# A decoder on one Trainium2 core: a new order of a block's work on all five queues, and the norms of queries and keys inverted one by one

## The chip, the cores and the metric

One core of a Trainium2 chip. The metric is the device time of one launch, in microseconds (us). The engines are TensorE (PE; its weight loads are PEld), VectorE (DVE), ScalarE (ACT), GpSimd (POOL) and SyncE (SP, which only issues DMAs). Each works through its own queue in order, and they meet at semaphores.

## The reference, cut to what matters

Three residual parts on x of shape (4, 512, 128): gated linear attention, cross attention, and a decoder of six layers. The change lies in the decoder. All in float32.

```
for i in range(6):
    x = attn_layer(shift_tokens(x), Wqkv[i], q_scale[i], k_scale[i], Wo[i]) + x
    x = ffn_layer(shift_tokens(x), ln_g[i], ln_b[i], W1[i], b1[i], W2[i], b2[i]) + x

attn_layer: q, k, v = split(x @ Wqkv)             # 16 heads of 64
            q = l2norm(q) * qs; k = l2norm(k) * ks # x / max(|x|, 1e-12), per head
            q, k = rotary(q), rotary(k)
            out = softmax(8 q k^T, masked) v       # windows of 32, this one and the last
            return out @ Wo
ffn_layer:  xn = layernorm(x) * g + b
            a, gate = split(xn @ W1 + b1)          # 341 each
            return a * gelu(gate) @ W2 + b2
```

## The kernel before, in words

The decoder works on blocks of 128 tokens: 4 blocks in a batch entry, 4 entries, 6 layers, so 96 blocks. `step(g, ...)` exists once for each engine and is called for g = 0 to 98. A step works on four blocks at once, as a pipeline: part a on block g (project, square, rotate and scale queries and keys), part b on block g-1 (values, turned keys and queries, scores and their maximum), part c on block g-2 (exponential, sums, turned weights, weighted values), part d on block g-3 (turn the heads' output). n = g % 4, and the entry that is four or more blocks behind is in its FFN: at n = 2 and 3 the output projection (`project_out`), at n = 0 the norm (`centre`, `variance`), at n = 1 the hidden layer (`hid_gate`, `hid_value`, `gelu`, `gated`, three chunks of 128, 128 and 85 channels), at n = 2 the second product (`ffn_project`, `update`). The FFN of entry f = g // 4 - 2 runs for g from 8 on. After the last step, `finish` does the last entry's FFN.

PSUM has four double banks: bank_x (values, then scores), bank_y (turned heads, turned keys, the keys' projection, weighted values), bank_z (the queries' projection, turned queries, turned weights), bank_f (the FFN). Each is used several times in a step, so an operation waits both for its inputs and for the last reader of its bank.

The order on PE in a step before: queries' projection (L683, through `project`, L609), values (L690), heads turned (L694, through `turn`, L613), FFN work, keys turned, queries turned (L709, L713), keys' projection (L718), half of the scores (L666), turned weights, the other half, FFN work, half of the weighing (L673), FFN work, the other half, and at n = 1 the third hidden chunk (L758). Waits there that matter: the keys' turn waits for POOL's product (`k_normed`) and for ACT's copy of the turned heads (`heads_turned_copied`); the queries' turn for `q_normed` and, since it overwrites bank_z, for DVE's rotation of the new queries (`q_sin`); the keys' projection for ACT's copy of the turned keys (`k_turned_copied`); the weighing for `k_sin`.

On ACT before: exponential of block g-2 (L958), at n = 1 the norm's affine (L944), square of the queries (L965), copy of the values (L970), of the turned heads (L977), mask (L981), at n = 0 the FFN's square (L932), at n = 1 the load of the GELU table (L985), copies of turned keys and queries (L990, L992), square of the keys (L1003), copy of the turned weights (L1008), at n = 0 the FFN's inverse spread (L936, L938), copy of the weighed heads (`copy_heads`, L950), and last both norms' logarithm and exponential in one pair of 32 columns (L1020, L1024). A norm is inverted as exp(-0.5 ln(max(sum, 1e-24))). At n = 1 the three GELUs (L926) lie between, and the load of the table of logarithm and exponential (L1017) before L1020.

On DVE before: row sums and reciprocal (L1126, L1130), rotation of the queries (`rotary`, L1080 and L1083, which first waits until POOL is done with the last block's queries, `q_normed`), their sum of squares (L1119), FFN work, rotation of the keys, maximum and shift of the scores (L1151, L1155), the keys' sum, and one clamp of both (L1162); then at n = 0 `norm` (L1108), at n = 3 `add_projected` (L1095 to L1101).

On POOL before: scaled weights (L1387), the queries' rotated sum (L1392), the next block's shifted tokens (`stage`, L1374, L1377), the keys' rotated sum (L1399), and then both products with the inverse norms (L1405), queries first.

SP issues the copies of the values into windows (`windows`, L354) when `values_copied` comes, and reloads weights at layer ends.

Of the kernel before, what the change touches and what calls it, by code (L numbers as in the profile page):

```python
# [7 lines left out]
PARTS = 128  # L8
# [21 lines left out]
def decoder(nc, io, LAYERS=6):  # L30
# [39 lines left out]
    sq_sums = sb('SS', [PARTS, 2, 16])  # L70
# [98 lines left out]
    sums_clamped = nc.alloc_semaphore('sums_clamped')  # L169
    norms_log = nc.alloc_semaphore('norms_log')  # L170
    inverse_norms = nc.alloc_semaphore('inverse_norms')
# [130 lines left out]
    alpha_w_loaded = nc.alloc_semaphore('alpha_w_loaded')  # L302
    HIDDEN_CHUNKS = [128, 128, 85]
# [11 lines left out]
    with nc.Block() as block:  # L315

        @block.sync
        def _(sp):
# [47 lines left out]
            sp.wait_ge(zeroed, 6)  # L366
# [27 lines left out]
        def _(pe):  # L394
# [221 lines left out]
            def hid_gate(k, R):  # L616
                M = HIDDEN_CHUNKS[k]
                mm(R[0:M, 0, :], w_1[:, 341 + k * 128:341 + k * 128 + M], ffn_in[:, :], start=True, stop=True)  # L618
# [37 lines left out]
            def step(g, n, a, b, c, d, f, fo):  # L656
# [19 lines left out]
                if a:  # L676
# [7 lines left out]
                    project(bank_z, w_q, 1, n).then_inc(q_projected, 1)  # L684
                if b:
# [62 lines left out]
                if f is not None and n == 1:  # L748
                    hid_value(1, bank_f)
# [48 lines left out]
        def _(act):  # L798
# [121 lines left out]
            def gelu(f, k, R):  # L920
                M = HIDDEN_CHUNKS[k]
                act.wait_ge(hidden_ready, 3 * f + k + 1)
# [17 lines left out]
            def ffn_affine(f):  # L940
                act.wait_ge(ffn_normed, f + 1)
                if due(f):
                    act.wait_ge(hidden_ready, 3 * f)
                A(ffn_in[:, :], normed[:, :], ACT.Identity, scale=layer_vecs[:, f // 4 * 9 + 6:f // 4 * 9 + 7], bias=layer_vecs[:, f // 4 * 9 + 7:f // 4 * 9 + 8]).then_inc(ffn_input, 1)  # L944

            def copy_heads(g):
# [3 lines left out]
                A(heads.rearrange('p (c q d) -> p q c d', q=2, d=64), bank_y.rearrange('p q (c d) -> p q c d', d=64), ACT.Copy).then_inc(heads_copied, 1)  # L950

            def step(g, n, a, b, c, d, f, fo):
# [6 lines left out]
                if f is not None and n == 1:  # L959
                    ffn_affine(f)  # L960
# [5 lines left out]
                if b:  # L966
                    act.wait_ge(values_ready, g)
                    if due(g - 1):
                        act.wait_ge(windows_loaded, 160 * (g - 1))
                    A(v_rows[:, (n - 1) % 2, :], flat(bank_x), ACT.Copy).then_inc(values_copied, 1)  # L970
                if d:
# [5 lines left out]
                    A(heads_t[:, :, slot * 128:slot * 128 + 128], turned(bank_y), ACT.Copy).then_inc(heads_turned_copied, 1)  # L977
                if b:
# [3 lines left out]
                if f is not None and n == 0:  # L982
                    square(f)
                if f is not None and n == 1:
                    nc.scalar.preload_act_table_set(GELU)  # L985
                if b:
# [3 lines left out]
                    A(k_t[:, :, 32 + 128 * par:160 + 128 * par], turned(bank_y), ACT.Copy).then_inc(k_turned_copied, 1)  # L990
                    act.wait_ge(q_turned, g)
                    A(q_t[:, :, :], turned(bank_z), ACT.Copy).then_inc(q_turned_copied, 1)  # L992
                    if n == 2:

                        act.wait_ge(k_turned_copied, g)
                        A(k_t[:, :, 0:32], k_t[:, :, 256:288], ACT.Copy).then_inc(keys_carried, 1)
                if f is not None and n == 1:
                    gelu(f, 0, bank_f)
                if a:
# [9 lines left out]
                if f is not None and n == 0:  # L1009
                    inverse(f)  # L1010
                if f is not None and n == 1:
                    gelu(f, 1, bank_f)
                if c:
                    copy_heads(g)
                if f is not None and n == 1:
                    gelu(f, 2, bank_f)
                    nc.scalar.preload_act_table_set(LNEXP)  # L1017
                if a:
                    act.wait_ge(sums_clamped, g + 1)
                    A(norm_logs[:, :], sq_clamped[:, :], ACT.Ln).then_inc(norms_log, 1)  # L1020
                    act.wait_ge(norms_log, g + 1)
                    if due(g):
                        act.wait_ge(k_normed, g)
                    A(inv_norms[:, :, :].rearrange('p a b -> p (a b)'), norm_logs[:, :], ACT.Exp, scale=-0.5).then_inc(inverse_norms, 1)  # L1024
# [11 lines left out]
            def finish():  # L1036
# [9 lines left out]
                ffn_affine(f)  # L1046
# [6 lines left out]
            act.wait_ge(zeroed, 6)  # L1053
# [8 lines left out]
        def _(dve):  # L1062
# [7 lines left out]
            def gated(f, k, R):  # L1070
                M = HIDDEN_CHUNKS[k]
                dve.wait_ge(gate_gelu, 3 * f + k + 1)
                if k == 0:
# [30 lines left out]
            def norm(f):  # L1104
                dve.wait_ge(ffn_inverse, f + 1)
                if due(f):
                    dve.wait_ge(ffn_input, f)
                V.tensor_tensor(normed[:, :], bank_f[:, 1, :], spread[:, :], ALU.mult).then_inc(ffn_normed, 1)  # L1108
# [6 lines left out]
            def sums(j, squared, done, g):  # L1115
# [377 lines left out]
```

## Time and profile before

| | |
|---|---|
| median of 3 runs | 2223.14 us (2221.44 to 2223.32) |
| the profiled execution | 2225.41 us, span 2223.6 us |
| PE busy | 2016.6 us, 91% of the span |
| DVE, ACT, POOL busy | 1359.7 (61%), 1357.9 (61%), 1079.4 us (49%) |
| mean granted TensorE clock | 0.984 |

The profile covers one execution. Its span runs from the first to the last instruction; its own time is 1.8 us longer. In the timeline a row merges like instructions that follow each other: its start is the first one's, its length reaches to the end of the last, and idle time in brackets lies ahead of it with what ended it. The end of a matmul is modelled and overlaps the next start, so distances are taken from start to start. A wait counts only where the waiting engine is what the others wait for.

### The profile page before, as it was taken

How to read it: one execution, taken by the hardware profiler on the slowest of the kernel's cores; microseconds unless marked ns; L12 is line 12 of the kernel's file. 1: busy time of each engine (PE TensorE's matmuls, PEld its weight loads, DVE VectorE, ACT ScalarE, POOL GpSimd, SP SyncE). 2: the span in 40 equal slices, each digit the busy share in tenths (PEclk: the TensorE clock that was granted, in tenths of full speed). 3: DMA queues.
4: the chain of work that ended last, by engine and by line, in shares of the span. 5: the costliest groups of instructions: out<-in, count | busy, mean ns of one | idle time of the engine just before them, and what ended most of it. 6: DMA issues, size and time to landing. Idle time of an engine off the chain costs nothing.

```text
span 2223.6 us, 73529 instructions
## 1 busy us (share of the span) xinstructions
PE 2016.6 (91%) x32616; PEld 1195.3 (54%) x32616; DVE 1359.7 (61%) x1663; ACT 1357.9 (61%) x1669; POOL 1079.4 (49%) x708
## 2 busy tenths in 40 slices
PE   8999997789999999999999999999999999999987
PEld 5655654355555555555555555555555555555553
DVE  1454454666666666666667666666666676667662
ACT  5556553456666666666666666666666666666664
POOL 0000000576555655565556555655555556556640
PEclk9999997799999999999999999999999999999999
DMA  3000000122223222232222322222322223222220
GB/s 105 1 1 1 1 20 29 39 59 59 59 60 86 68 68 59 59 89 69 67 59 69 86 59 76 72 57 69 78 70 68 59 59 88 68 69 59 59 59 19
DMA packets 82055, 128.02 MB, mean 58 GB/s; under 512 B 17230, under 2 KB 28108, under 8 KB 81740
## 3 DMA queue, kind: packets, MB, share of 16 engines
q1 hardware_dynamic: 81740, 123.33, 21.4%
q8 instruction: 258, 4.23, 0.8%
q14 instruction: 57, 0.47, 0.1%
HBM read 21.55 MB, written 1.05 MB: 10 GB/s over the span
## 4 chain that ended last, share of the span: by engine, by line
PE 64%; ACT 16%; issue 8%; DVE 7%; POOL 4%; DMA 0%; POOLq 0%; ACTq 0%; SPq 0%; DVEq 0%
PE ps L609 14%; PE ps L613 8%; PE ps L635 7%; PE ps L673 5%; PE ps L690 5%; PE ps L666 5%; ACT KT L990 4%; PE ps L422 3%; PE ps L653 3%; PE ps L618 2%; PE ps L622 2%; POOL work L1405 2%; DVE work L1083 2%; DVE work L1080 2%; ACT ps L981 2%
## 5 line engine op out<-in xcount | busy, mean ns | idle before, releaser
L1405 POOL TENSOR_TENSOR work<-work,RS 128x1024 f32<-128x1024 f32 x192 | 361.6, 1904 | 312.4 <-ACT RS L1024 312.4
L613 PEld LDWEIGHTS ps<-ident,work 128*128 128x128 f32 x3072 | 346.8, 142 | 150.6 <-issue 71.0
L1080 DVE TENSOR_TENSOR work<-ps,work 128x1024 f32<-128x1024 f32 x192 | 230.7, 1202 | 314.3 <-ACT work L1003 303.0
L613 PE MATMUL ps<-ident,work 128*128 128x128 f32 x3072 | 396.6, 277 | 27.9 <-POOL work L1405 12.5
L1399 POOL TENSOR_TENSOR work<-work 128x1024 f32<-128x1024 f32 x96 | 226.2, 2356 | 372.8 <-DVE work L1083 372.8
L609 PE MATMUL ps<-WK,XS 128*128 128x512 f32 x384 | 190.8, 620 | 50.0 <-ACT KT L990 49.8
L1083 DVE TENSOR_TENSOR work<-ps,work 128x1024 f32<-128x1024 f32 x192 | 233.0, 1214 | 0.0
L1119 DVE TENSOR_REDUCE SS<-work 128x16 f32<-128x1024 f32 x192 | 232.0, 1209 | 0.0
L1392 POOL TENSOR_TENSOR work<-work 128x1024 f32<-128x1024 f32 x96 | 226.1, 2356 | 5.7 <-DVE work L1083 5.7
L950 ACT ACTIVATE work<-ps 128x1024 f32<-128x1024 f32 x96 | 98.1, 1022 | 210.0 <-PE ps L673 208.2
L673 PEld LDWEIGHTS ps<-work 64*32 64x32 f32 x12288 | 135.4, 105 | 165.4 <-issue 109.2
L673 PE MATMUL ps<-work 64*32 64x64 f32 x12288 | 171.5, 224 | 33.9 <-DVE work L1083 18.0
L609 PE MATMUL ps<-WQ,XS 128*128 128x512 f32 x384 | 193.3, 626 | 8.5 <-POOL XS L1377 4.3
L635 PE MATMUL ps<-work,WO 128*128 128x512 f32 x384 | 193.3, 617 | 0.0
L1126 DVE TENSOR_REDUCE LE<-work 128x16 f32<-128x1024 f32 x96 | 116.9, 1218 | 123.5 <-ACT work L958 123.2
L666 PEld LDWEIGHTS ps<-KT,work 64*32 64x32 f32 x12288 | 135.9, 105 | 104.6 <-issue 102.9
L1387 POOL TENSOR_TENSOR work<-work,RL 128x1024 f32<-128x1024 f32 x96 | 182.9, 1905 | 11.9 <-DVE RL L1130 11.9
L690 PE MATMUL ps<-WV,XS 128*128 128x512 f32 x384 | 181.8, 596 | 2.5 <-DVE work L1155 2.5
L666 PE MATMUL ps<-KT,work 64*32 64x64 f32 x12288 | 171.1, 224 | 11.8 <-issue 11.4
L1003 ACT ACTIVATE work<-ps 128x1024 f32<-128x1024 f32 x96 | 98.5, 1026 | 95.5 <-PE ps L609 95.5
L1417 POOL TENSOR_TENSOR work<-work 128x512 f32<-128x512 f32 x16 | 16.5, 1041 | 273.7 <-PE ps L456 148.1
L1076 DVE SCALAR_TENSOR_TENSOR work<-ps,vec,work 128x512 f32<-128x512 f32 (+1 forms) x72 | 53.8, 747 | 150.4 <-ACT work L926 150.4
(183 smaller groups left out, 3097.8 us busy)
## 6 DMA issues: line engine op xcount, KB each, us to landing
work<-work SPq DMA_DIRECT2D x576, 128.0 KB
work<-work SPq DMA_DIRECT2D x336, 64.0 KB
WQ<-in_wqkv SPq DMA_DIRECT2D x6, 512.0 KB, 3.6
WK<-in_wqkv SPq DMA_DIRECT2D x6, 512.0 KB, 4.0
WV<-in_wqkv SPq DMA_DIRECT2D x6, 512.0 KB, 3.7
WO<-in_wo SPq DMA_DIRECT2D x6, 512.0 KB, 3.9
work<-ZR SPq DMA_DIRECT2D x48, 64.0 KB
W<-in_w SPq DMA_DIRECT2D x6, 341.0 KB, 3.0
```

The costliest lines, as they stand in the source:

```text
L609: return mm(R[:, half, :], x_shift[:, 32 + at * 128:160 + at * 128], w[:, half * 512:half * 512 + 512], start=True, stop=True)
L613: m = nc.tensor.transpose(flat(R)[:, t * 128:t * 128 + 128], src[:, t * 128:t * 128 + 128], ident[:, :])
L635: m = mm(bank_f[:, 0, :], w_o[:, k, :], heads_t[:, k, 128 * (f % 2):128 * (f % 2) + 512], start=k == 0, stop=k == 7)
L666: m = mm(bank_x[32 * w:32 * w + 32, q, c8 * 64:c8 * 64 + 64], q_t[64 * q:64 * q + 64, c8, 32 * w:32 * w + 32], k_t[64 * q:64 * q + 64, c8, ...
L673: m = mm(bank_y[32 * w:32 * w + 32, q, c8 * 64:c8 * 64 + 64], probs_t[64 * q:64 * q + 64, c8, 32 * w:32 * w + 32], v_win[64 * q:64 * q + 6 ...
L690: m = mm(bank_x[:, q, :].rearrange('p (c d) -> p c d', d=64), x_shift[:, 32 + nb * 128:160 + nb * 128], w_v[:, :].rearrange('p (c q d) -> ...
L1080: V.tensor_tensor(h16(cos_part[:, j, :]), h16(flat(src)), rotary_tabs[:, at:at + 64].unsqueeze(1).broadcast_to([PARTS, 16, 64]), ALU.mult) ...
L1083: V.tensor_tensor(halves(sin_part[:, j, :]), halves(flat(src))[:, :, ::-1, :], rotary_tabs[:, at + 256:at + 320].rearrange('p (s d) -> p s ...
L1119: V.tensor_reduce(sq_sums[:, j, :], h16(squares[:, j, :]), AX, ALU.add).then_inc(done, 1)
L1392: U.tensor_tensor(cos_part[:, 0, :], cos_part[:, 0, :], sin_part[:, 0, :], ALU.add).then_inc(q_rotated, 1)
L1399: U.tensor_tensor(cos_part[:, 1, :], cos_part[:, 1, :], sin_part[:, 1, :], ALU.add).then_inc(k_rotated, 1)
L1405: U.tensor_tensor(h16(qk_norm[:, j, :]), h16(cos_part[:, j, :]), inv_norms[:, j, :].unsqueeze(2).broadcast_to([PARTS, 16, 64]), ALU.mult). ...
```

## The change

PE: the heads are turned before the values are projected, and the keys are turned right after the values, ahead of the FFN work; the queries' turn and the keys' projection stay behind it. At n = 1 the second hidden chunk's gate and value are done together, the third chunk's gate goes between the halves of the weighing (with a wait for the second GELU), its value stays last. The GELU waits for the gate's product alone. ACT: the inversion of the norms is split in two, each of 16 columns; the queries' goes ahead of the keys' square (at n = 1 with an FFN: into the next step, behind the copy of the turned heads), the keys' goes ahead of `copy_heads`, except at n = 1; the copy of the turned heads goes ahead of that of the values; the GELU table is loaded behind the copy of the turned keys; at n = 0 the FFN's inverse goes last. The norm's affine goes from ACT to DVE. DVE: each clamp is a maximum over pairs (sum, 1e-24), done right after its sum; at n = 1 the second `gated` goes behind the scores' shift. POOL: the queries' product goes ahead of the keys' rotated sum (at n = 1 with an FFN: behind the keys' product). SP issues what it did, in the same order.

```diff
@@ PE @@
+                if d:
+                    pe.wait_ge(heads_copied, g - 2)
+                    turn(bank_y, heads).then_inc(heads_turned, 1)
                 if b:
...
                     m.then_inc(values_ready, 1)
-                if d:
-                    pe.wait_ge(heads_copied, g - 2)
-                    turn(bank_y, heads).then_inc(heads_turned, 1)
+                if b:
+                    pe.wait_ge(k_normed, g)
+                    if d:
+                        pe.wait_ge(heads_turned_copied, g - 2)
+                    turn(bank_y, qk_norm[:, 1, :]).then_inc(k_turned, 1)
                 if f is not None and n == 0:
                     centre(f)
...
                 if b:
-                    pe.wait_ge(k_normed, g)
-                    if d:
-                        pe.wait_ge(heads_turned_copied, g - 2)
-                    turn(bank_y, qk_norm[:, 1, :]).then_inc(k_turned, 1)
                     if a:
                         pe.wait_ge(q_sin, g + 1)
...
                     pe.wait_ge(hidden_gated, 3 * f + 1)
-                    hid_gate(1, bank_f)
+                    hid(1, bank_f)
...
-                    hid_value(1, bank_f)
+                    pe.wait_ge(gate_gelu, 3 * f + 2)
+                    hid_gate(2, bank_f)
...
                     pe.wait_ge(hidden_gated, 3 * f + 2)
-                    hid(2, bank_f)
+                    hid_value(2, bank_f)
@@ ACT @@
+            def invert_norms(g, j):
+                clamped, logs, inverse_done, normed_ = ((q_clamped, q_norms_log, q_inverse, q_normed), (k_clamped, k_norms_log, k_inverse, k_normed))[j]
+                act.wait_ge(clamped, g + 1)
+                A(norm_logs[:, 16 * j:16 * j + 16], sq_clamped[:, 16 * j:16 * j + 16], ACT.Ln).then_inc(logs, 1)
...
+                A(inv_norms[:, j, :], norm_logs[:, 16 * j:16 * j + 16], ACT.Exp, scale=-0.5).then_inc(inverse_done, 1)
...
-                if f is not None and n == 1:
-                    ffn_affine(f)
...
+                if n == 2 and f is not None and g - 1 < ALL_BLOCKS:
+                    invert_norms(g - 1, 0)
+                if b:
+                    act.wait_ge(values_ready, g)
...
                 if f is not None and n == 1:
                     gelu(f, 0, bank_f)
+                elif a:
+                    invert_norms(g, 0)
                 if a:
                     act.wait_ge(k_projected, g + 1)
...
                 if f is not None and n == 1:
                     gelu(f, 1, bank_f)
+                    gelu(f, 2, bank_f)
                     copy_heads(g)
                     nc.scalar.preload_act_table_set(LNEXP)
+                    if a:
+                        invert_norms(g, 1)
+                elif f is not None and n == 0:
+                    if c:
+                        copy_heads(g)
+                    if a:
+                        invert_norms(g, 1)
+                    inverse(f)
+                else:
+                    if a:
+                        invert_norms(g, 1)
+                    if c:
+                        copy_heads(g)
@@ DVE @@
-                V.tensor_tensor(normed[:, :], bank_f[:, 1, :], spread[:, :], ALU.mult).then_inc(ffn_normed, 1)
+                V.scalar_tensor_tensor(out=bank_f[:, 0, :], in0=bank_f[:, 1, :], scalar=layer_vecs[:, f // 4 * 9 + 6:f // 4 * 9 + 7], in1=spread[:, :], op0=ALU.mult, op1=ALU.mult).then_inc(ffn_normed, 1)
+                dve.wait_ge(ffn_normed, f + 1)
+                V.tensor_scalar(ffn_in[:, :], bank_f[:, 0, :], layer_vecs[:, f // 4 * 9 + 7:f // 4 * 9 + 8], None, ALU.add).then_inc(ffn_input, 1)
...
-                V.tensor_reduce(sq_sums[:, j, :], h16(squares[:, j, :]), AX, ALU.add).then_inc(done, 1)
+                V.tensor_reduce(sq_sums[:, j, :, 0], h16(squares[:, j, :]), AX, ALU.add).then_inc(done, 1)
+                dve.wait_ge(done, g + 1)
+                if due(g):
+                    dve.wait_ge(logs, g)
+                V.tensor_reduce(sq_clamped[:, 16 * j:16 * j + 16], sq_sums[:, j, :, :], AX, ALU.max).then_inc(clamped, 1)
@@ POOL @@
+                    late = f is not None and n == 1
+                    if not late:
+                        norm_product(g, 0)
                     pool.wait_ge(k_cos, g + 1)
...
+                    norm_product(g, 1)
+                    if late:
+                        norm_product(g, 0)
```

`norm_product(g, j)` is the body of the old loop at L1405 with the wait on the half's own inverse. One more constant is set at the start (1e-24 beside each sum).

## Rows read from the trace of the kernel before

**Rows 1.** The page: the chain that ended last, by engine.
```profile
PE 64%; ACT 16%; issue 8%; DVE 7%; POOL 4%; DMA 0%; POOLq 0%; ACTq 0%; SPq 0%; DVEq 0%
```
**Rows 2.** A wait over the whole span: waiter, releaser, us in total, times, longest.
```profile
PE ps L609 <- ACT KT L990: 49.8, 83, 1.3
```
**Rows 3.** Timeline of PE: start us, us, engine, line, out<-in, xcount, idle before.
```profile
645.79 1.88 PE L609 MATMUL ps<-WQ,XS 128*128 128x512 f32 x4
...
1161.62 1.88 PE L609 MATMUL ps<-WQ,XS 128*128 128x512 f32 x4
...
1170.75 1.96 PE L609 MATMUL ps<-WK,XS 128*128 128x512 f32 x4 [0.33 <-ACT KT L990]
...
1179.78 1.98 PE L609 MATMUL ps<-WQ,XS 128*128 128x512 f32 x4
...
1183.31 1.04 PE L613 MATMUL ps<-ident,work 128*128 128x128 f32 x8
...
1197.18 1.98 PE L609 MATMUL ps<-WQ,XS 128*128 128x512 f32 x4
...
1204.33 1.09 PE L613 MATMUL ps<-ident,work 128*128 128x128 f32 x8 [0.26 <-DVE work L1083]
1205.35 1.96 PE L609 MATMUL ps<-WK,XS 128*128 128x512 f32 x4
...
1210.81 0.86 PE L673 MATMUL ps<-work 64*32 64x64 f32 x64 [0.73 <-DVE work L1083]
...
1213.82 1.98 PE L609 MATMUL ps<-WQ,XS 128*128 128x512 f32 x4
...
1223.19 1.96 PE L609 MATMUL ps<-WK,XS 128*128 128x512 f32 x4 [1.32 <-ACT KT L990]
...
1232.20 1.09 PE L618 MATMUL ps<-YN,W 128*85 128x512 f32 x2 [0.78 <-DVE work L1076]
...
1233.99 1.88 PE L609 MATMUL ps<-WQ,XS 128*128 128x512 f32 x4
...
2115.00 1.88 PE L609 MATMUL ps<-WQ,XS 128*128 128x512 f32 x4
```
**Rows 4.** Timeline of ACT around the starts of steps.
```profile
1197.29 1.02 ACT L950 ACTIVATE work<-ps 128x1024 f32<-128x1024 f32 x1 [3.45 <-PE ps L673]
...
1212.76 0.69 ACT L936 ACTIVATE YQ<-ps,tiny 128x512 f32<-128x512 f32 x1 [2.58 <-PE ps L647]
...
1214.02 1.00 ACT L950 ACTIVATE work<-ps 128x1024 f32<-128x1024 f32 x1
...
1234.89 1.28 ACT L1017 ACT_TABLE_LOAD   x1
1236.19 0.23 ACT L1020 ACTIVATE LS<-SL 128x32 f32<-128x32 f32 x1
...
1236.58 1.04 ACT L958 ACTIVATE work<-work 128x1024 f32<-128x1024 f32 x1
...
1238.43 1.02 ACT L970 ACTIVATE work<-ps 128x1024 f32<-128x1024 f32 x1
```
**Rows 5.** Timeline of DVE: clamps, and from the row sums to the queries' rotation.
```profile
1182.49 1.22 DVE L1126 TENSOR_REDUCE LE<-work 128x16 f32<-128x1024 f32 x1 [2.55 <-ACT work L958]
...
1185.00 1.21 DVE L1083 TENSOR_TENSOR work<-ps,work 128x1024 f32<-128x1024 f32 x1
...
1198.02 0.18 DVE L1162 TENSOR_SCALAR SL<-SS 128x32 f32<-128x32 f32 x1
...
1214.36 0.18 DVE L1162 TENSOR_SCALAR SL<-SS 128x32 f32<-128x32 f32 x1
```
**Rows 6.** Timeline of POOL: the two norm products of a step.
```profile
1236.75 3.77 POOL L1405 TENSOR_TENSOR work<-work,RS 128x1024 f32<-128x1024 f32 x2 [5.63 <-ACT RS L1024]
```
**Rows 7.** Groups by line over the span: mean ns of one, then idle before.
```profile
L1113 DVE SCALAR_TENSOR_TENSOR X<-ps,vec,X 128x512 f32<-128x512 f32 x24 | 17.8, 742 | 6.6 <-PE ps L653 6.6
```
**Rows 8.** Timeline of PE in step 6, where the clock fell.
```profile
502.85 3.50 PE L613 MATMUL ps<-ident,work 128*128 128x128 f32 x16 [2.17 <-POOL work L1405]
```

More of the change, by code:

```diff
@@ L981, in step @@
                     A(bank_x.rearrange('p q (c k) -> p (q c) k', k=64), seed.unsqueeze(1).broadcast_to([PARTS, 16, 64]), ACT.Copy).then_inc(mask_seeded, 1)
[L982 to L985, printed above, removed]
                 if b:
@@ L990, in step @@
                     A(k_t[:, :, 32 + 128 * par:160 + 128 * par], turned(bank_y), ACT.Copy).then_inc(k_turned_copied, 1)
+                if f is not None and n == 1:
+                    nc.scalar.preload_act_table_set(GELU)
+                if b:
                     act.wait_ge(q_turned, g)
@@ L996, in step @@
                         A(k_t[:, :, 0:32], k_t[:, :, 256:288], ACT.Copy).then_inc(keys_carried, 1)
+                if f is not None and n == 0:
+                    square(f)
                 if f is not None and n == 1:
                     gelu(f, 0, bank_f)
+                elif a:
+                    invert_norms(g, 0)
                 if a:
@@ L1113, in update, with sums @@
                 V.scalar_tensor_tensor(out=xc, in0=bank_f[:, 1, :], scalar=layer_vecs[:, f // 4 * 9 + 8:f // 4 * 9 + 9], in1=xc, op0=ALU.add, op1=ALU.add).then_inc(x_updated, 1)
-            def sums(j, squared, done, g):
+            def sums(j, g):
+                squared, done, clamped, logs = ((q_squared, q_sums, q_clamped, q_norms_log), (k_squared, k_sums, k_clamped, k_norms_log))[j]
                 dve.wait_ge(squared, g + 1)
                 if due(g):
-                    dve.wait_ge(sums_clamped, g)
-                V.tensor_reduce(sq_sums[:, j, :], h16(squares[:, j, :]), AX, ALU.add).then_inc(done, 1)
+                    dve.wait_ge(clamped, g)
+                V.tensor_reduce(sq_sums[:, j, :, 0], h16(squares[:, j, :]), AX, ALU.add).then_inc(done, 1)
+                dve.wait_ge(done, g + 1)
+                if due(g):
+                    dve.wait_ge(logs, g)
+                V.tensor_reduce(sq_clamped[:, 16 * j:16 * j + 16], sq_sums[:, j, :, :], AX, ALU.max).then_inc(clamped, 1)
             def step(g, n, a, b, c, d, f, fo):
@@ L1136, in step @@
                     rotary(g, n, 0, bank_z, q_cos, q_sin, q_rotated)
-                    sums(0, q_squared, q_sums, g)
+                    sums(0, g)
                 if f is not None and n == 2:
@@ L1146, in step @@
                     rotary(g, n, 1, bank_y, k_cos, k_sin, k_rotated)
-                if f is not None and n == 1:
-                    gated(f, 1, bank_f)
                 if b:
@@ L1155, in step @@
                     V.tensor_tensor(scores_sb[:, :, :, :], by_head(bank_x), per_head(row_max[:, :]).unsqueeze(3).broadcast_to([PARTS, 8, 2, 64]), ALU.subtract).then_inc(scores_shifted, 1)
+                if f is not None and n == 1:
+                    gated(f, 1, bank_f)
                 if a:
-                    sums(1, k_squared, k_sums, g)
-                    dve.wait_ge(q_sums, g + 1)
-                    dve.wait_ge(k_sums, g + 1)
-                    if due(g):
-                        dve.wait_ge(norms_log, g)
-                    V.tensor_scalar(sq_clamped[:, :], sq_sums[:, :, :].rearrange('p a b -> p (a b)'), 1e-24, None, ALU.max).then_inc(sums_clamped, 1)
+                    sums(1, g)
                 if f is not None and n == 0:
@@ L1351, in _ @@
             cross()
+            dve.wait_ge(zeroed, 7)
             for g in range(ALL_BLOCKS + 3):
@@ L1381, in scale_tables, with norm_product @@
                 U.tensor_tensor(t, rotary_base[:, :, :, :], qk_scales[:, :, layer, :].unsqueeze(2).broadcast_to([PARTS, 4, 4, 64]), ALU.mult).then_inc(tables_scaled, 1)
+            def norm_product(g, j):
+                inverse_done, turned, rotated, normed_ = ((q_inverse, q_turned, q_rotated, q_normed), (k_inverse, k_turned, k_rotated, k_normed))[j]
+                pool.wait_ge(inverse_done, g + 1)
+                pool.wait_ge(rotated, g + 1)
+                if due(g):
+                    pool.wait_ge(turned, g)
+                U.tensor_tensor(h16(qk_norm[:, j, :]), h16(cos_part[:, j, :]), inv_norms[:, j, :].unsqueeze(2).broadcast_to([PARTS, 16, 64]), ALU.mult).then_inc(normed_, 1)
             def step(g, n, a, b, c, d, f, fo):
@@ L1399, in step @@
                     U.tensor_tensor(cos_part[:, 1, :], cos_part[:, 1, :], sin_part[:, 1, :], ALU.add).then_inc(k_rotated, 1)
-                    for j, (turned, rotated, normed_) in enumerate(((q_turned, q_rotated, q_normed), (k_turned, k_rotated, k_normed))):
-                        pool.wait_ge(inverse_norms, g + 1)
-                        pool.wait_ge(rotated, g + 1)
-                        if due(g):
-                            pool.wait_ge(turned, g)
-                        U.tensor_tensor(h16(qk_norm[:, j, :]), h16(cos_part[:, j, :]), inv_norms[:, j, :].unsqueeze(2).broadcast_to([PARTS, 16, 64]), ALU.mult).then_inc(normed_, 1)
+                    norm_product(g, 1)
+                    if late:
+                        norm_product(g, 0)
             def attention():
```

55 lines of the change are left out of this document (21 added, 34 removed).

## The prediction

> **What bounds the kernel now.** First the page's chain: 64% of it is PE, 16% ACT, 7% DVE, 4% POOL [rows 1]. So PE sets the time, and what can be won are its waits on the others; the largest by name is the keys' projection behind ACT's copy of the turned keys, 49.8 us over 83 cases [rows 2]. Second, PE's timeline, read from one queries' projection to the next [rows 3]. Steps with n = 2, 3, 0, 1 take 18.16, 17.40, 16.64 and 20.17 us, 72.37 together. From 645.79 to 2115.00 there are 20 such rounds, 73.46 us each, so the round shown is a fair one. Its waits: 0.33 us each at n = 2 and 3, about 1.4 at n = 0 (0.73 of it ahead of the weighing, for DVE's `k_sin`), about 2.1 at n = 1 (1.32 ahead of the keys' projection, 0.78 ahead of the third hidden chunk) [rows 3]. The passes themselves stay, so the change can win 4 us a round at the very most, 90 us over the 22 rounds with an FFN. Third, the other engines' timelines around a step's start: who hands what to whom, and when [rows 4 to 6].
>
> I place the changed order on a clock that starts (t = 0) at the queries' projection, with these distances. PE: queries and values 3.53 us together, then a turn 0.89, so the values are through at t = 4.42 with the heads turned first; a queries' turn 1.02 before the keys' projection [rows 3]. ACT: copies of 1024 columns follow each other by 0.93, a logarithm and its exponential take 0.39 to the next instruction, table load to logarithm 1.30 [rows 4]. From a copy's end to the matmul it releases I take 0.14. DVE: end of the exponential (1182.44) to the end of the queries' rotation (1186.21) 3.75 us [rows 5]; there the exponential began 1.05 before DVE's row. POOL: one product 1.90, half of the pair [rows 6].
>
> **Step n = 3 (gain 0.2).** The keys' sum is clamped just at t = 0, so its inversion ahead of `copy_heads` delays that copy from 0.1 to 0.6, and its end, 1.6, is in time for the heads' turn at 1.8. Exponential 1.55, square 2.5, copy of the heads 3.4 to 4.4, keys' turn at 4.56. `k_normed` comes at 0.7 + 1.9 = 2.6: in time. From the end of the values to the keys' projection the old step needs the same turns and passes. It stood at 9.23 with 0.33 of waiting, 8.90 without; the new one stands at 9.05. The rest is equal, 8.17: **17.22 against 17.40**.
>
> **Step n = 0 (loss 0.2).** Here the clamp comes at t = 0.84 [rows 5], `copy_heads` behind the inversion at 1.5 instead of 0.1 [rows 4], and the heads are turned at 2.64, 0.8 late. The exponential starts at 2.4 against 1.45, ends at 3.45; DVE is busy with the residual adds until about then anyway, so the queries' rotation ends at 7.2 against 7.1. The queries' turn needs it, at 7.15 before and 7.25 now, then the copy of the turned keys (8.2 + 0.14) holds the keys' projection to 8.34 against 8.17. The queries' inversion, 0.5 us now ahead of the keys' square, ends at 10.3 where that square may begin at 10.3: free, by a hair. `k_sin` and the weighing move with the projection: **16.84 against 16.64**. The second, small clamp for the queries (0.18 by the old clamp's row, 0.3 with its wait) lies in DVE's idle time before the keys' rotation.
>
> **Step n = 1 (gain 0.6).** ACT begins with `copy_heads` 0.1; the inversion waits for the clamp (0.54 before [rows 5], 0.9 without the 0.38 by which the last weighing was held up) and ends at 1.65; the FFN's inverse spread, once ahead of the copy, takes 1.26 up to the next instruction [rows 4], so the exponential starts at 2.8, the square 3.75, the copy of the heads 4.7 to 5.7, and the keys' turn, free at 4.42, waits until 5.82. From there: turn 0.89, first hidden chunk 1.73, queries' turn 1.02, keys' projection at 9.46, against 9.37: moving the table load and the affine buys nothing there. Behind the projection the old step needs 10.80 with 0.78 of waiting [rows 3]; that wait goes, since the second GELU now follows the gate and has the weighing as cover, and one more change between passes costs 0.08: 10.10. **19.56 against 20.17**. The affine (ACT) becomes two instructions of DVE, at most 0.75 each by the nearest row of PSUM operands [rows 7]. They start at 2.95, end by 4.5, and push the row sums to at most 4.5 from 3.9; the rotation then ends near 8.2, and the queries' turn comes at 8.44: hidden, with 0.2 to spare.
>
> **Step n = 2 (loss 1.2), the decisive one.** The queries' inversion of the step before is issued here, behind the copy of the turned heads. ACT: `copy_heads` from -0.96, table load 0.08 to 1.36, the keys' inversion 1.38, exponential 1.77, square 2.7, copy of the heads 3.6 to 4.65, then the queries' logarithm and exponential, done at 5.05. POOL's product runs 5.08 to 7.0. DVE's rotation of the new queries waits for it (`q_normed`): it would have begun at 4.4, begins at 7.0, and ends 2.3 later, 9.3. The keys' turn stands at 4.77, and with the old 4.50 of work from there to the keys' projection (9.13 less 4.30 less 0.33 [rows 3]) PE would be at the queries' turn at 8.25; it waits until 9.35 instead, for `q_sin`. Keys' projection 10.37, rest 9.03: **19.40 against 18.16**. The old kernel had both products done at 1240.52, t = 6.5, but with only POOL's pair between, and DVE started at 5.1, as soon as the first was done.
>
> The table load's price decides how late this is. Its row lasts 1.28 and the logarithm follows 1.30 after its start [rows 4]. The Trainium skill, page "ScalarE: Activation LUTs", section "What ACT_TABLE_LOAD costs", adds a drain and gives about 2.66 us for a switch; by it step 2 would end 1.4 us later and the kernel some 30 us. The sum is by the row.
>
> **The rest.** The keys' product is queued before the queries' in POOL at n = 1 only; elsewhere the queries' goes ahead of `k_sin` in idle time, behind `stage`, whose shifted tokens are needed five us later. The values' copy, and with it SP's ten window DMAs, starts 0.6 to 1.6 later; they are awaited only at the next step's weighing, over 10 us on. Steps without an FFN at the start: the keys' product comes 1.9 earlier, the exponential 0.9 later; I count nothing, with 4 us to either side. In the last step and `finish` the GELUs no longer wait for the value pass, 0.4 to 0.9 each in two places: 1.5 us gained. Two more small instructions on ACT a step (0.39 together) and one on DVE are in the times above.
>
> **Sum.** A round: 17.22 + 16.84 + 19.56 + 19.40 = 73.02 against 72.37, +0.65. Times 22: +14.3; less 1.5: +12.8 us. The profiled execution took 2225.4 us, 2.3 above the median; from the median I get **2236 us**.
>
> **Rivals.**
> *A, the late queries cost nothing net (faster).* Place: PE's queues. The mean round is 1.09 us longer than the one shown, through short gaps within runs of small matmuls, not on the path of DVE and ACT. The changed order waits 5.2 us a round on those engines (2.1, 1.4, 1.6 and 0.1) against 4.2, so more of such gaps fall where PE would wait anyway. It decides once 0.65 us a round is absorbed; if all 1.09 is, and the n = 3 and n = 1 gains stand, the result is -0.44 x 22 - 1.5 = -11: 2212 us. Against it: a gap is absorbed only where PE is not what the others wait for; one ahead of the keys' projection delays DVE's chain as well.
> *B, the handover is as walked but tighter elsewhere (slower still).* At n = 0 and n = 1 three margins of 0.0 to 0.2 us stand; if all fail, 0.4 a round more, +9: 2245.
> *C, the clock.* In step 6 PE waited 2.17 us, and 16 turns then took 3.50 us where they take 1.91: the lower level of 1.2 GHz [rows 8]. The new waits are 0.8 to 1.4, and a wait of 1.32 at n = 1 did not bring it [rows 3], so I give this little. Once a round at 1.7 us: +37, 2273. The Trainium skill, page "TensorE: Matmul & The Clock Gate", has the clock follow recent activity; the trace agrees with that in step 6.
> *D, no net effect:* the walk's errors, 0.1 to 0.2 a step, cancel the 0.65: 2223.
>
> **Numbers.** Forecast with B 0.62, A 0.22, D 0.11, C 0.05. Range 2208 to 2256: A at its lower end to B with the start's 4 us and half of C. About 0.2% (4.4 us) is what a measurement of this kernel can tell from no change. Faster 0.24, same 0.13, slower 0.63.
>
> **What would show it.** Right: at n = 2 a DVE wait of about 2.5 us before the queries' rotation with POOL as releaser, a PE wait of about 1.1 before the queries' turn on DVE, step lengths near 19.4, 17.2, 16.8, 19.6; at n = 1 PE waiting about 1.4 us for the copy of the turned heads, and no wait before the third chunk's value. At n = 0 a wait of 0.8 before the heads' turn. Wrong: n = 2 under 18.4, a clock that falls in steady rounds, or n = 1 not shorter.

## The result, and the profile after

The changed kernel takes 2236.51 us (median of 7 runs, 2230.06 to 2239.68) against 2221.86 us for the kernel before on the same chip; the ratio is 1.0066, 95% interval 1.0056 to 1.0077. It is slower by about 15 us, with the forecast at 2236. That the number is met so closely is luck: two errors in the sum, of 18 and 20 us, cancel, as the part on the prediction works out. The step that it called decisive came as described.

The page of the changed kernel: span and instructions, busy time, and the chain that ended last by engine, which answers to [rows 1].

```profile
span 2234.7 us, 74105 instructions
...
PE 2017.7 (90%) x32616; PEld 1181.3 (53%) x32616; DVE 1398.5 (63%) x1783; ACT 1379.7 (62%) x1837; POOL 1090.2 (49%) x709
...
PE 61%; ACT 16%; issue 11%; DVE 10%; POOL 2%; DMA 0%; POOLq 0%; DVEq 0%; ACTq 0%; SPq 0%
```

PE does the same 32616 matmuls in the same busy time (2017.7 against 2016.6 us), so 10 of the 11 us of span are idle time. In the chain POOL fell from 4% to 2% and DVE rose from 7% to 10%; "issue", time in which an engine waited for nothing the profile shows, rose from 8% to 11%.

The timeline of PE in one round of the changed kernel, n = 2, 3, 0, 1 (start, length, line, what, idle before), with the starts of the first and the last of 20 rounds around it; it answers to [rows 3]. L613 with WQ is the queries' projection, L617 a turn, L613 with WK the keys' projection, L677 the weighing.

```profile
643.36 1.88 PE L613 MATMUL ps<-WQ,XS 128*128 128x512 f32 x4
...
1161.35 1.88 PE L613 MATMUL ps<-WQ,XS 128*128 128x512 f32 x4
...
1166.25 1.07 PE L617 MATMUL ps<-ident,work 128*128 128x128 f32 x8 [0.42 <-ACT work L980]
...
1170.98 1.09 PE L617 MATMUL ps<-ident,work 128*128 128x128 f32 x8 [1.09 <-DVE work L1098]
1171.91 1.88 PE L613 MATMUL ps<-WK,XS 128*128 128x512 f32 x4
...
1180.87 1.98 PE L613 MATMUL ps<-WQ,XS 128*128 128x512 f32 x4
...
1189.66 1.88 PE L613 MATMUL ps<-WK,XS 128*128 128x512 f32 x4
...
1197.83 1.98 PE L613 MATMUL ps<-WQ,XS 128*128 128x512 f32 x4
1200.19 1.09 PE L617 MATMUL ps<-ident,work 128*128 128x128 f32 x8 [0.38 <-ACT work L950]
...
1206.23 1.95 PE L613 MATMUL ps<-WK,XS 128*128 128x512 f32 x4 [0.24 <-ACT KT L996]
...
1211.69 0.86 PE L677 MATMUL ps<-work 64*32 64x64 f32 x64 [0.78 <-DVE work L1098]
...
1214.70 1.98 PE L613 MATMUL ps<-WQ,XS 128*128 128x512 f32 x4
...
1220.34 1.06 PE L617 MATMUL ps<-ident,work 128*128 128x128 f32 x8 [1.06 <-ACT work L980]
...
1223.83 1.88 PE L613 MATMUL ps<-WK,XS 128*128 128x512 f32 x4
...
1233.68 1.88 PE L613 MATMUL ps<-WQ,XS 128*128 128x512 f32 x4
...
2123.51 1.88 PE L613 MATMUL ps<-WQ,XS 128*128 128x512 f32 x4
```

The four steps shown take 19.52, 16.96, 16.87 and 18.98 us, 72.33 together: as much as the 72.37 of the round shown before. But the mean over 20 rounds is (2123.51 - 643.36) / 20 = 74.01 against 73.46. So the loss is not in the round one happens to look at; it is in what varies from round to round. Taken over all full steps between 600 and 2115 us, with PE's idle time that has no releaser ("gaps") beside it:

| mean step, us (shortest) | n = 0 | n = 1 | n = 2 | n = 3 | round | gaps in a round |
|---|---|---|---|---|---|---|
| before | 16.80 (16.25) | 20.61 (20.11) | 18.33 (18.15) | 17.73 (17.40) | 73.47 | 1.02 |
| changed | 16.69 (15.88) | 19.66 (18.98) | 19.96 (19.51) | 17.74 (16.83) | 74.05 | 1.93 |

The shortest steps add to 71.91 before and 71.20 now, but they don't fall in one round: of the 20 rounds no one is shorter than 72.37 before and 72.33 now. The waits with a named releaser became fewer (86 to 77 us over 620 to 2115 us), and the gaps doubled (21 to 40 us). The two groups of waits that carry most of the gaps, over 620 to 2115 us, first in the kernel before (waiter, releaser, us in total, times, longest), where L666 is the scores and L673 the weighing:

```profile
PE ps L673 <- issue: 12.1, 21, 1.5
...
PE ps L666 <- issue: 8.7, 16, 1.1
```

and the same stretch in the changed kernel, where the scores are L670 and the weighing L677:

```profile
PE ps L670 <- issue: 25.3, 28, 1.6
...
PE ps L677 <- issue: 10.7, 19, 1.0
```

Both lines are the bursts of 64 small matmuls. The scores' gaps tripled.

The decisive step n = 2, as it came. ACT in the changed kernel, from the table load on: L956 and L960 are a logarithm and an exponential, L980 the copy of the turned heads between the keys' pair and the queries'.

```profile
1161.57 1.28 ACT L1026 ACT_TABLE_LOAD   x1
1162.87 0.22 ACT L956 ACTIVATE LS<-SL 128x16 f32<-128x16 f32 x1
...
1165.09 1.01 ACT L980 ACTIVATE work<-ps 128x1024 f32<-128x1024 f32 x1
...
1166.24 0.22 ACT L960 ACTIVATE RS<-LS 128x16 f32<-128x16 f32 x1
```

POOL, keys' product and then queries':

```profile
1163.41 1.90 POOL L1408 TENSOR_TENSOR work<-work,RS 128x1024 f32<-128x1024 f32 x1 [4.24 <-ACT RS L960]
1166.53 1.91 POOL L1408 TENSOR_TENSOR work<-work,RS 128x1024 f32<-128x1024 f32 x1 [1.22 <-ACT RS L960]
```

and DVE, the row sums and the rotation of the new queries:

```profile
1164.31 1.22 DVE L1149 TENSOR_REDUCE LE<-work 128x16 f32<-128x1024 f32 x1 [1.94 <-ACT work L968]
...
1168.57 1.23 DVE L1095 TENSOR_TENSOR work<-ps,work 128x1024 f32<-128x1024 f32 x1 [2.75 <-POOL work L1408]
```

The inversion ends at t = 5.1, the product at 7.1, the rotation starts at 7.2 (walked: 5.05, 7.0, 7.0), after a wait of 2.75 us (walked: about 2.5), and PE waits 1.09 us for it; its queries' turn comes at 9.63 (walked: 9.35).

### The profile page after: what moved, and what is told of

It is laid out like the page before. It is cut to its first block, busy times and chain, and to the rows that moved or that the text cites. A ratio compares the mean times of both kernels' runs of the same rounds, so it can differ in the third digit from the quotient of the medians.

```text
span 2234.7 us, 74105 instructions
## 1 busy us (share of the span) xinstructions
PE 2017.7 (90%) x32616; PEld 1181.3 (53%) x32616; DVE 1398.5 (63%) x1783; ACT 1379.7 (62%) x1837; POOL 1090.2 (49%) x709
## 4 chain that ended last, share of the span: by engine, by line
PE 61%; ACT 16%; issue 11%; DVE 10%; POOL 2%; DMA 0%; POOLq 0%; DVEq 0%; ACTq 0%; SPq 0%
PE ps L613 11%; PE ps L617 10%; PE ps L639 7%; PE ps L677 6%; PE ps L670 4%; PE ps L697 4%; PE ps L426 3%; PE ps L622 3%; DVE work L1098 3%; DVE work L1095 2%; ACT work L973 2%; PE ps L626 2%; POOL work L1408 2%; ACT work L980 2%; ACT work L1016 2%
## 5 line engine op out<-in xcount | busy, mean ns | idle before, releaser
L617 PEld LDWEIGHTS ps<-ident,work 128*128 128x128 f32 x3072 | 343.3, 142 | 271.2 <-issue 114.0
L617 PE MATMUL ps<-ident,work 128*128 128x128 f32 x3072 | 411.8, 277 | 76.1 <-ACT work L980 32.9
L677 PEld LDWEIGHTS ps<-work 64*32 64x32 f32 x12288 | 135.6, 105 | 164.6 <-issue 123.4
L613 PE MATMUL ps<-WQ,XS 128*128 128x512 f32 x384 | 194.8, 630 | 10.3 <-POOL XS L1396 4.1
L670 PEld LDWEIGHTS ps<-KT,work 64*32 64x32 f32 x12288 | 137.9, 105 | 123.2 <-issue 121.0
L677 PE MATMUL ps<-work 64*32 64x64 f32 x12288 | 171.5, 224 | 32.2 <-DVE work L1098 17.3
L670 PE MATMUL ps<-KT,work 64*32 64x64 f32 x12288 | 174.4, 224 | 28.7 <-issue 28.6
L613 PE MATMUL ps<-WK,XS 128*128 128x512 f32 x384 | 185.4, 606 | 10.6 <-ACT KT L996 10.6
L956 ACT ACTIVATE LS<-SL 128x16 f32<-128x16 f32 x192 | 40.9, 213 | 237.6 <-DVE SL L1142 237.3
```

What stands on the lines that cost most here:

```text
L613: return mm(R[:, half, :], x_shift[:, 32 + at * 128:160 + at * 128], w[:, half * 512:half * 512 + 512], start=True, stop=True)
L617: m = nc.tensor.transpose(flat(R)[:, t * 128:t * 128 + 128], src[:, t * 128:t * 128 + 128], ident[:, :])
L670: m = mm(bank_x[32 * w:32 * w + 32, q, c8 * 64:c8 * 64 + 64], q_t[64 * q:64 * q + 64, c8, 32 * w:32 * w + 32], k_t[64 * q:64 * q + 64, c8, ...
L677: m = mm(bank_y[32 * w:32 * w + 32, q, c8 * 64:c8 * 64 + 64], probs_t[64 * q:64 * q + 64, c8, 32 * w:32 * w + 32], v_win[64 * q:64 * q + 6 ...
```

## The experiments

Ratios are to the kernel before, measured beside it on the same chip. The changed kernel's 1.0066 is the one given with the result, from other runs; differences to it are taken between ratios, 0.001 being 2.2 us.

**e1: the late queries' inversion moved.**

```diff
                     if a:
                         invert_norms(g, 1)
+                        invert_norms(g, 0)
                 elif f is not None and n == 0:
...
-                if n == 2 and f is not None and g - 1 < ALL_BLOCKS:
-                    invert_norms(g - 1, 0)
```

> The changed kernel, but the queries' inversion of the n = 1 steps is issued at the end of that step, right behind the keys' inversion, not in the next step behind the copy of the turned heads. Theory (the late queries' product is what costs step n = 2 its 1.1 us wait for the rotation): POOL's two products then run back to back, the second is done 1.2 us earlier; the exponential of step 2 and the copy of the turned heads come 0.5 later. Wait for the rotation 1.1 to about 0.1 to 0.3, step n = 2 0.8 to 0.9 shorter, kernel -18 us against the changed one, about 2218. Rival (DVE's rotation is late for another reason, the row sums): -0 to -4 us.

Measured 2212.66 us, ratio 0.9979 (0.9969 to 0.9990), so 19 us less than the changed kernel. Step n = 2 is 19.05 on average against 19.96, the other three within 0.1 of theirs. The wait for the rotation ahead of the queries' turn is gone from the list (it was 21.7 us over 20 cases); the turns' remaining wait is ACT's copy of the turned heads:

```profile
PE ps L617 <- ACT work L980: 39.3, 42, 1.1
```

The theory stands, in mechanism and size: the place of one pair of 0.2 us instructions on ACT cost 0.9 us a round, more than the 0.58 that the whole change lost. The gaps at n = 2 hardly rose with it (0.36 to 0.41).

**e2: the hidden layer's part alone, on the kernel before.**

```diff
-                    hid_gate(1, bank_f)
+                    hid(1, bank_f)
...
-                    hid_value(1, bank_f)
+                    pe.wait_ge(gate_gelu, 3 * f + 2)
+                    hid_gate(2, bank_f)
...
-                    hid(2, bank_f)
+                    hid_value(2, bank_f)
...
-                act.wait_ge(hidden_ready, 3 * f + k + 1)
+                act.wait_ge(gates_ready, 3 * f + k + 1)
```

> The kernel before, with only the hidden layer's part of the change: GELU waits for the gate's product, the second chunk's gate and value together, the third chunk's gate between the halves of the weighing. Theory (this part took away the 0.67 us wait of n = 1 ahead of the third chunk): that wait goes to 0, step n = 1 0.6 to 0.7 shorter, kernel -13 to -15 us, about 2209. Rival (the wait hid PE's short gaps without a releaser, 0.18 us a step at n = 1 before and 0.54 after): the gaps at n = 1 rise to about 0.5 and the gain is halved, -6 to -9 us.

Measured 2198.12 us, 0.9910 (0.9895 to 0.9925), -19 us. Step n = 1 is 19.69 against 20.61: the 0.67 of waiting is gone, and 0.25 more. The gaps at n = 1 did not rise (0.18 before, 0.10 now), so the rival was wrong here: the wait that went was not the one that hid gaps.

**e6: as e2, and the GELU table loaded behind the copy of the turned keys.** It is told here since it is the other half of the pair.

```diff
-                if f is not None and n == 1:
-                    nc.scalar.preload_act_table_set(GELU)
...
                     A(k_t[:, :, 32 + 128 * par:160 + 128 * par], turned(bank_y), ACT.Copy).then_inc(k_turned_copied, 1)
+                    if f is not None and n == 1:
+                        nc.scalar.preload_act_table_set(GELU)
```

> The kernel before with the hidden layer's part of the change (as e2) and the GELU table loaded behind the copy of the turned keys. Theory W (a wait just ahead of the keys' projection gives the instruction queue time, so PE's gaps without a releaser come back where such a wait goes): the wait of 1.29 us ahead of the keys' projection at n = 1 falls to 0.2 or less, the gaps at n = 1 rise from 0.10 to 0.4 or more, the step gets 0.6 to 0.8 shorter, kernel 0.984 to 0.986 of the one before. Rival (the gaps come from the keys' turn ahead of the FFN work): gaps at n = 1 stay at 0.1, the step gets 1.0 shorter, 0.981.

Measured 2193.64 us, 0.9882 (0.9865 to 0.9900). The waits of PE in e2, where L610 is the keys' projection, L667 the scores and L674 the weighing:

```profile
PE ps L610 <- ACT KT L992: 45.5, 74, 1.3
...
PE ps L674 <- issue: 8.6, 14, 1.5
PE ps L667 <- issue: 7.1, 15, 0.7
```

and in e6:

```profile
PE ps L610 <- ACT KT L990: 24.9, 73, 0.4
PE ps L667 <- issue: 22.2, 39, 1.9
...
PE ps L674 <- issue: 10.4, 20, 1.6
```

The wait ahead of the keys' projection gave back 20.6 us (45.5 to 24.9), and the scores' gaps took 15.1 (7.1 to 22.2). At n = 1 the wait fell from 1.29 to 0.33 and the gaps rose from 0.10 to 0.86: of 0.96 us only 0.13 reached the mean step (19.69 to 19.56), while the shortest step fell by 0.5 (19.21 to 18.69). Theory W named the 0.4 or more; the gain was even smaller than it said. Between the whole kernels the step from e2 to e6 is 0.0028, 6 us, with intervals of 0.0015 and 0.0018 to either side. This also answers the rival: the keys' turn stands where it stood, so these gaps don't come from turning the keys early, but go with the shorter wait ahead of the keys' projection.

**e9 and e10: a quarter of the small matmuls, in the kernel before and in the changed one.** Left out in both: scores and weighted values of three windows of four.

```diff
-                            for w in range(4):
...
-                                m = mm(bank_x[32 * w:32 * w + 32, q, c8 * 64:c8 * 64 + 64], q_t[64 * q:64 * q + 64, c8, 32 * w:32 * w + 32], k_t[64 * q:64 * q + 64, c8, kc:kc + 64], start=False, stop=True, skip_group_check=True)
+                            m = mm(bank_x[:, q, c8 * 64:c8 * 64 + 64], q_t[64 * q:64 * q + 64, c8, :], k_t[64 * q:64 * q + 64, c8, 128 * par0:128 * par0 + 64], start=False, stop=True, skip_group_check=True)
```

and `weigh` alike.

> The kernel before with a quarter of the matmuls in the scores and in the weighing: one matmul of 128 queries in place of four of 32, against the first window's keys and values alone (the other windows' scores and values are left out). PE's bursts keep about their length but hold a quarter of the instructions. Theory F (PE's gaps without a releaser are late instructions in bursts of small matmuls): the gaps fall from 1.0 us a round to 0.1 or less, the steps come to stand at their shortest lengths of before, 16.3, 20.1, 18.2 and 17.4, each within 0.2 if the bursts keep their length. Rival (gaps of another origin): gaps stay.

> The changed kernel with the same cut of the small matmuls as in e9. Theory F: gaps fall from 1.9 us a round to 0.1 or less, steps at their shortest, 15.9, 19.0, 19.5 and 16.8, 71.2 a round against 72.0 for e9; so the changed order is then faster than the old one by about 0.7 us a round, 15 us, and the sign of the change turns. Rival (the changed order loses by its waits alone, as predicted): it stays slower than e9 by 10 us or more.

Measured 2262.09 us (1.0201, 1.0184 to 1.0218) and 2252.92 us (1.0162, 1.0147 to 1.0177). The instruction queue's row on the page of e9, which read 258 packets in both full kernels:

```profile
q8 instruction: 114, 1.87, 0.3%
```

PE's timeline in e9 from one queries' projection to the next, with the new burst between:

```profile
1168.28 1.88 PE L609 MATMUL ps<-WQ,XS 128*128 128x512 f32 x4
...
1179.30 1.11 PE L664 MATMUL ps<-KT,work 64*128 64x64 f32 x16
...
1187.45 1.98 PE L609 MATMUL ps<-WQ,XS 128*128 128x512 f32 x4
```

A burst of 16 takes 1.04 us to the next start where 64 small ones took 0.79, so the steps did not come to stand at their old shortest lengths: a burst is 0.25 longer, which makes each kernel slower as a whole, and the two are to be compared with each other. But not one gap is left in either: every step of a kind is as long as the next to 0.01 us. The rounds are 75.38 us (16.76, 21.05, 19.16, 18.41) before and 74.74 us (16.38, 19.99, 20.53, 17.84) after, and the changed order is the faster one by 9.2 us. With the gaps gone, the sign of the change turns. The rival, my own forecast's ground, fails: the changed order does not lose by its waits.

The size of 9.2 us holds for these bursts alone, since a longer burst covers waits as well: the wait ahead of the third chunk at n = 1 is 0.53 in e9 where it was 0.78, and the wait for the copy of the heads at n = 0 is gone in e10 where it was 0.38. In the full kernels the rounds nearest to having no gaps are 72.37 and 72.33 us, which shows that the loss goes with the gaps, but hardly a gain.

**e3: the copy of the weighed heads ahead of the keys' inversion at n = 2 and 3.**

```diff
                 else:
+                    if c:
+                        copy_heads(g)
                     if a:
                         invert_norms(g, 1)
-                    if c:
-                        copy_heads(g)
```

> The changed kernel with the copy of the weighed heads ahead of the keys' inversion at n = 2 and 3 as well. Theory (the clamp at 0.84 us of n = 0 delays the copy and with it the heads' turn by 0.4, and the exponential): step n = 0 0.2 shorter, n = 2, 3 and 1 unchanged, steps without an FFN up to 0.5 shorter each, kernel -4 to -7 us. Rival (the keys' product, 0.5 to 0.9 later, becomes the wait ahead of the keys' turn): n = 0 and n = 3 longer, +5 us or more.

Measured 2220.15 us, 1.0019 (1.0000 to 1.0039), 10 us less than the changed kernel. Step n = 0 is 16.41 against 16.69, the others shorter by 0.02 to 0.10. Direction and place as expected, the size above the range.

**e4: window DMAs later, in the kernel before.**

```diff
                 sp.wait_ge(values_copied, m + 1)
+                sp.wait_ge(mask_seeded, m + 1)
```

> The kernel before with the window DMAs of each block held until the mask is written, about 2 us later, as late and later than in the changed kernel. Theory (PE's gaps without a releaser end 2.0 to 2.9 us after a packet of the instruction queue starts, and those packets take longer beside the windows' packets): PE's gaps rise from 1.0 us a round towards 1.9, kernel +5 to +18 us. Rival (the gaps come from the order of waits on PE, not from the DMAs): gaps stay near 1.0 a round, kernel within 2 us of the one before.

Measured 2226.01 us, 1.0034 (1.0022 to 1.0047): slower, as the theory said. But the trace does not carry it. The gaps are 0.84 a round, no more than before, and the round is 73.47. The theory's step is refuted, and where the 7.5 us lie stays open.

**e5: three moves on ACT in the changed kernel.** The edits of e1 and e3, and the copy of the turned heads (L980) ahead of the queries' square (L973), two blocks changing places.

> The changed kernel with three moves on ScalarE: the queries' inversion at the end of the n = 1 step, the copy of the weighed heads ahead of the keys' inversion, and the copy of the turned heads ahead of the queries' square. Theory (after the first two, what holds PE at n = 1 and 2 is the keys' turn, 1.07 and 0.79 us behind the copy of the turned heads, and the square stands in the way for nothing): the waits fall to about 0.15 and 0.1, steps near 18.1 and 18.0, n = 3 and n = 0 near 16.9 and 16.0 plus PE's gaps of 1.9 a round; kernel near 0.985 of the one before. Rival (DVE's rotation needs the square and is then the wait, and the gaps grow as waits go): 0.995 or more.

Measured 2209.27 us, 0.9955 (0.9938 to 0.9972): the rival, in time and mechanism; only the gaps hardly grew (2.14 us a round against 1.93). The waits of turns on PE:

```profile
PE ps L617 <- DVE work L1097: 38.3, 61, 1.0
...
PE ps L617 <- ACT work L975: 2.4, 12, 0.2
```

The wait for the copy of the heads is gone (39.3 us in e1), and DVE's rotation, which needs the square, took its place with 38.3. n = 0 is 16.87 with 1.66 us of waiting for DVE, where e3 had 16.41.

**e7: the norm's affine on ACT again, in the changed kernel.** `ffn_affine` as before behind L968, `norm` on DVE as before.

> The changed kernel with the norm's affine on ScalarE again, behind the exponential of n = 1, and one product on DVE. Theory (ACT's row of copies decides n = 1): the keys' turn waits about 0.7 us longer, 1.8 against 1.07, step n = 1 0.7 longer, kernel +12 to +16 us against the changed one, about 1.013 of the one before. Rival (DVE's second instruction cost as much as it saved): within 3 us of the changed kernel.

Measured 2243.94 us, 1.0112 (1.0093 to 1.0130), 10 us more than the changed kernel. The wait of the keys' turn at n = 1 is 1.78 us against 1.07, and the shortest step 0.70 longer, both as said. The mean step is only 0.58 longer.

**e8: the kernel before again**, profiled on the chip of e5 to e7.

> The kernel before, once more with a profile on the chip that runs the others. It should show the step lengths, waits and gaps of the first profile: rounds of 73.5 us with 1.0 us of gaps. If its gaps come near 1.9, the gaps say nothing about the order.

2217.34 us (one run), rounds of 73.31 us with 0.86 of gaps: the gaps belong to the order.

**e11: e1 and e3 together.**

> The changed kernel with the two moves of e1 and e3 together. If they are independent: -19.5 and -10 us against the changed kernel, 0.993 of the one before. If the gaps take back part of it, as in e5: 0.996.

Measured 2201.81 us, 0.9929 (0.9914 to 0.9944): they add. The changed order, with two small things put right on ACT, is faster than the kernel before by 16 us (0.0071 of 2218).

**e12: e6 with the affine on DVE.**

> Kernel e6 with the norm's affine on DVE as in the change. ACT is 0.7 us lighter at n = 1, so the last 0.33 us ahead of the keys' projection there goes, down to the floor of PE's work. Theory F: gaps take it back, the step stays at 19.5 on average, ratio 0.987 to 0.989, the same as e6. Rival (waits add up plainly): n = 1 0.3 shorter, 0.985.

Measured 2192.27 us, 0.9882 (0.9867 to 0.9897), the ratio of e6. But the reason given is not what happened: the wait ahead of the keys' projection at n = 1 stayed at 0.33, with gaps of 0.84, while the step got shorter, 19.38 against 19.56 (4 us in 22 rounds, within the two intervals). e6 and e12 are the fastest versions run, 26 us below the kernel before; both keep the old order of turns and the old, unsplit norms.

## Why the prediction was right, and where it was not

*The decisive step* (n = 2, loss 1.2 from the queries' late product): right. Walked 19.40, seen 19.52, with each hand-over within 0.3 us; e1 takes the cause away and gets 0.9 of it back in the mean. One reading behind it was wrong: the old rotation did not start as soon as POOL's first product was done, at about 1238.65 (half of the pair in [rows 6]), but at 1239.08, when DVE's own reciprocal was through.

*n = 0* (16.84): right for the round shown, 16.87 with the last weighing 0.38 late in both kernels; the waits for the copy of the heads (0.38 instead of 0.8) and for the keys' copy came where they were put. In the mean of 21 steps the loss of 0.2 is not there: 16.80 before, 16.69 now. DVE's sum-to-clamp distance is 1.24 instead of 1.30, and the clamp 0.18 as taken.

*n = 1 and n = 3* (19.56 and 17.22): direction right, gain too small. Seen 18.98 and 16.96. The terms that were mis-sized are mostly distances between PE's groups: a queries' turn that does not wait takes 0.87 to the keys' projection, not 1.02 (that was read behind a wait), in both steps; at n = 1 a projection that follows a turn directly takes 1.81 to the scores, not 1.88, and the hidden layer's new order costs 0.1 less than the old one, not 0.08 more. At n = 3 the keys' turn came at 4.44, not 4.56. At n = 1 it came at 5.64, not 5.82, since the clamp and with it the keys' inversion and the exponential came earlier: the inversion ended at 1.48 (walked 1.65), the exponential began at 2.63 (walked 2.8), with the step's start at 1214.70.

```profile
1215.97 0.21 ACT L960 ACTIVATE RS<-LS 128x16 f32<-128x16 f32 x1
...
1217.33 1.04 ACT L968 ACTIVATE work<-work 128x1024 f32<-128x1024 f32 x1
```

Together 0.84 us a round, 18 us in 22 rounds. In the mean n = 3 gained nothing (17.73 and 17.74), its gaps having grown from 0.18 to 0.49, and n = 1 gained 0.95.

*The table load*: by the row, 1.28 and 1.30 to the next instruction, and so it is after: the load at 1161.57, the logarithm at 1162.87. By the page "ScalarE: Activation LUTs" of the Trainium skill, section "What ACT_TABLE_LOAD costs", about 2.66 us for a switch, the sum would have been higher by an estimated 30 us; the trace does not agree with that figure, and the measurement decides.

*Sum*: with those terms right, the walk gives 72.2 against 72.37 a round, and the forecast would have been no change or a slight gain. What made up for it is the gaps, which the sum had as unchanged. They went from 1.02 to 1.93 us a round, 20 us in 22 rounds, more than the whole loss. So the sign of the forecast rests on a term that was not in it, and the number on luck. That the late product alone costs 19 us and is worth fixing is shown by e1; that the loss goes away with the gaps, and the sign with it, by e9 against e10.

*Rival A* had the gaps in view, but its premise did not come: it had the changed order waiting 5.2 us a round against 4.2 and so absorbing more of them. In the rounds shown it waits 3.97 (1.51, 0, 1.40, 1.06) against 4.14, less and not more. It also seems to matter where a wait stands. The change took waiting away right ahead of the keys' projection (0.33 at n = 2 and 3, 1.32 at n = 1 [rows 3]), and the gaps rose in just these steps (0.09 to 0.36, 0.18 to 0.49, and 0.18 to 0.54), not at n = 0 (0.58 to 0.54); e6 did the same at n = 1 alone, with the same outcome. The wait of 1.09 that e1 took away stood one group earlier, ahead of the queries' turn, and gave its time back. Why the place should matter is not shown.

*Rival B* (margins failing): no, in the round shown no step is longer than walked by more than 0.12. *Rival C* (clock): the granted clock is 0.984 over the span in both kernels and 1.00 from 643 to 2115 us, with waits of 1.09 and 1.06 in each round. *The ends*: the changed kernel enters the first full round 2.4 us earlier (643.36 against 645.79), inside the 4 us allowed; behind the last one it takes 2.6 us more (111.2 against 108.6), of which 1.35 is the last n = 2 step. Forecast was 1.5 gained. One cause that shows is the clock: its granted mean over the last 74 us is 0.86 against 0.93 before. PE waited 2.21 us, and the turn and the last values' projection behind it took 1.52 and 3.19 us where 1.09 and 1.88 are usual; from 2163.60 to 2166.90 the granted clock was 0.60, so much of that stretch was at the lower level.

```profile
2162.34 1.52 PE L617 MATMUL ps<-ident,work 128*128 128x128 f32 x8 [2.21 <-ACT work L950]
2163.65 3.19 PE L697 MATMUL ps<-WV,XS 128*128 128x512 f32 x4
```

How much of the tail it costs was not tried.

## What to carry to other kernels

Walk a reordered pipeline hand-over by hand-over against the in-order queues: it found the one late pair of small instructions that cost more than the rest of the change brought. But compare means over many rounds, not one clean round, before calling a wait a cost: a wait ahead of a dense burst of small instructions may be paying for the burst's instructions to arrive, and taking it away then brings little of what it shows (0.13 of 0.96 us a step in e6). Another wait gave back all of its time (e1, e2), so it has to be tried. And take distances from rows in the same state, behind a wait or not.

## What was not expected of the hardware

PE's short stops inside runs of small matmuls look like late instructions. Between 620 and 2115 us all 38 stops before (21 us) and all 50 in the changed kernel (40 us) end 2.2 to 3.2 us after the last start of a packet of the instruction queue, by the times as recorded, while those packets come 7.5 us apart on average. And the stops go with the instructions: 258 packets with 64 matmuls a burst, 114 packets and no stop with 16. That run also changed the shape of the matmuls, so the number of instructions is not the only thing it changed. The packets last 1.11 us on average before and 1.17 after; whether the windows' packets beside them matter stays open, since e4 moved those and found no more stops.
